# The last attention's scores as three f32r products of high and low parts, with fewer slots

## The reference

```python
q = _split_heads(xn @ Wq)                      # 16 heads of 64
kv = xn @ Wkv
k = _split_heads(kv[..., :INNER]); v = _split_heads(kv[..., INNER:])
mem = _split_heads(memories @ Wm)              # memories: the context
k = jnp.concatenate([k, mem], axis=2)          # 100 own keys + 722
v = jnp.concatenate([v, mem], axis=2)
dots = jnp.einsum('bhid,bhjd->bhij', q, k) * scale
attn = jax.nn.softmax(dots, axis=-1)
out = jnp.einsum('bhij,bhjd->bhid', attn, v)
return out.transpose(0, 2, 1, 3).reshape(b, n, h * d) @ Wo + bo
```

## Time and profile before

| | us |
|---|---|
| median of three runs | 1789.09 |
| the profiled execution | 1776.6 |
| its span | 1774.9 |
| TensorE matmuls busy | 1598.0 (90%) |
| TensorE weight loads busy | 1370.2 (77%) |
| VectorE busy | 1088.9 (61%) |
| ScalarE busy | 787.0 (44%) |
| GpSimd busy | 185.0 (10%) |

### The profile page before, as it was taken

One profiled execution on the slowest core, in us unless ns is written; L12 is line 12 of the kernel. 1 busy time (PEld: TensorE's weight loads), 2 busy tenths in 40 slices (PEclk: granted clock), 3 DMA queues, 4 the chain that ended last, 5 costly groups with the idle time before them and its releaser, 6 DMA issues. The chain is left out here.

```text
span 1774.9 us, 31782 instructions
## 1 busy us (share of the span) xinstructions
PE 1598.0 (90%) x11904; PEld 1370.2 (77%) x11904; DVE 1088.9 (61%) x2045; ACT 787.0 (44%) x1418; POOL 185.0 (10%) x172
## 2 busy tenths in 40 slices
PE   6998399999999399799999999999999749999990
PEld 5786289988888399588787787878787449999990
DVE  3687567777777633246565565656565557767774
ACT  2445255555555332144444354535444325445541
POOL 1103201111111101100000000000000030011003
PEclk9998599999999799899999999999999869999995
DMA  6995356666667434231110112021112046666643
GB/s 192 370 401 196 103 216 216 219 213 204 216 205 236 131 114 145 87 102 34 35 49 23 50 27 58 19 58 36 40 36 75 11 147 210 203 205 197 219 158 90
DMA packets 93125, 246.00 MB, mean 139 GB/s; under 512 B 32870, under 2 KB 39526, under 8 KB 77926
## 3 DMA queue, kind: packets, MB, share of 16 engines
q1 hardware_dynamic: 82534, 219.87, 36.7%
q0 software_dynamic: 10496, 24.81, 5.9%
HBM read 179.14 MB, written 65.50 MB: 138 GB/s over the span
## 5 line engine op out<-in xcount | busy, mean ns | idle before, releaser
L1848 PE MATMUL banks<-a_ch,a_wm 128*128 128x362 f32 (+1 forms) x1024 | 285.7, 340 | 9.4 <-DVE a_cl L2009 9.4
L1172 DVE TENSOR_TENSOR e_lo<-e_raw,e_hi 128x2048 fp32r<-128x2048 f32 x98 | 225.5, 2301 | 91.1 <-ACT e_hi L1250 91.0
L1123 PE MATMUL banks<-e_xh,e_hi 128*128 128x256 f32 x768 | 215.9, 281 | 4.2 <-DVE e_xl L1188 4.2
L1123 PE MATMUL banks<-e_xl,e_hi 128*128 128x256 f32 x768 | 215.7, 281 | 0.0
L1123 PE MATMUL banks<-e_xh,e_lo 128*128 128x256 f32 x768 | 215.2, 280 | 0.0
L1250 ACT CAST e_hi<-e_raw 128x2048 fp32r<-128x2048 f32 x98 | 186.5, 1903 | 29.0 <-PE banks L1102 29.0
L1848 PEld LDWEIGHTS banks<-a_ch,a_wm 128*128 128x128 f32 x1024 | 186.2, 190 | 11.1 <-DVE a_cl L2009 10.5
L1848 PE MATMUL banks<-a_cl,a_wm 128*128 128x362 f32 (+1 forms) x512 | 168.8, 330 | 0.0
L2022 DVE TENSOR_REDUCE a_nmax<-banks 100x1 f32<-100x822 f32 x128 | 123.5, 1007 | 72.2 <-PE banks L1882 72.2
L1102 PE MATMUL banks<-e_hi,e_hh 128*128 128x512 f32 x384 | 153.8, 400 | 1.5 <-DVE e_hl L1208 1.5
L1123 PEld LDWEIGHTS banks<-e_xh,e_hi 128*128 128x128 f32 x768 | 145.1, 189 | 10.6 <-issue 4.6
(11 more groups left out here) (270 smaller groups left out, 3052.4 us busy)
## 6 DMA issues: line engine op xcount, KB each, us to landing
e_raw<-wout SPq DMA_DIRECT2D x50, 1024.0 KB, 15.5
e_raw<-w SPq DMA_DIRECT2D x34, 1024.0 KB, 22.4
slot_rows<-a_zero SPq DMA_DIRECT2D x66, 514.0 KB, 9.8
e_raw<-wgate SPq DMA_DIRECT2D x17, 1024.0 KB
e_raw<-wup SPq DMA_DIRECT2D x17, 1024.0 KB, 4.9
a_craw<-ctxT SPq DMA_DIRECT2D x32, 361.0 KB, 6.4
e_xs<-slot_rows SPq DMA_DIRECT2D x18, 514.0 KB, 3.7
p_raw<-Wkv SPq DMA_DIRECT2D x4, 1024.0 KB, 12.0
```

The lines of the kernel that those rows point to most:

```text
L1123: mm = nc.tensor.matmul(ps[:, bank, 0:CAP], w[:, cc, cut], x[:, cc, :], start=t == 0, stop=t == len(terms) - 1)
L1172: nc.vector.tensor_tensor(lo[g % 2][i], raw[q % RAW][:], hi[g % 2][i].bitcast(F32), ALU.subtract)\
L1848: mm = nc.tensor.matmul(ps[:, 6 + half, 0:wide], w[:, cc, cut], x[:, cc, start:start + wide], start=cc == 0 and t == 0, stop=cc == DC - 1 ...
```

## The change

The scores are taken as three f32r products: high part by high part, high by low, low by high, all three for one width before the next width, the heads in turn. For this the pair's queries and keys are kept as a high and a low tile of 100 + 822 columns (`qk_hi`, `qk_lo`), in two slots. The projected rows stand once more in f32 (`mem`), from which `turn_values` reads. New work for each pair:

- GpSimd (`own_split`): a copy of the own queries and keys (128x200) to the high tile, and the subtraction that makes the low part. SyncE loads them to a tile of their own (`own_qk`), two pairs ahead where it was three.
- ScalarE: in `keys` the first half of the projected rows is copied out of the bank twice, to the high tile and to `mem`; `keys_second`, after the values' copies, makes the high part of the second half out of `mem`.
- VectorE (`keys_low`): after `keys` it waits for the high part and subtracts 128x722.

Values and probabilities have three slots in place of four. GpSimd's routing work is now spread over the steps, behind the step's `own_split`.

```diff
-    SLOTS = 4
+    QK_SLOTS, V_SLOTS, P_SLOTS = 2, 3, 3
+    MEMORY = 2 * T
...
+                def own_queries_keys(p):
                     if not exists(p):
                         return
-                    after(sp, sc, p - SLOTS + 1)
...
+                    b, m, s = p // IC, p % IC, p % QK_SLOTS
+                    after(sp, own_lo, p - QK_SLOTS + 1)
+                    sp.dma_start(own_qk[s][:, 0, :], s1.q[b, :, m, :]).then_inc(qk_in[s], 16)
+                    sp.dma_start(own_qk[s][:, 1, :], s1.kk[b, :, m, :]).then_inc(qk_in[s], 16)
+
+                def own_values(p):
+                    if not exists(p):
+                        return
+                    b, m, s = p // IC, p % IC, p % V_SLOTS
+                    after(sp, yd, p - V_SLOTS + 1)
+                    sp.dma_start(v[s][0:T, 0, :], s1.v[b, :, 128 * m:128 * m + 128]).then_inc(v_in[s], 16)
...
-                    own(b, m + SLOTS - 1)
+                    own_queries_keys(IC * b + m + 2)
+                    own_values(IC * b + m + 2)
...
+                def own_split(p):
+
+                    s = p % QK_SLOTS
+                    raw = own_qk[s][:].rearrange("p a t -> p (a t)")
+                    pool.wait_ge(qk_in[s], 32 * (p // QK_SLOTS + 1))
+                    after(pool, sc, p - QK_SLOTS + 1)
+                    pool.tensor_copy(qk_hi[s][:, 0:MEMORY], raw).then_inc(own_hi, 1)
+                    pool.wait_ge(own_hi, p + 1)
+                    pool.tensor_tensor(qk_lo[s][:, 0:MEMORY], raw, qk_hi[s][:, 0:MEMORY].bitcast(F32), ALU.subtract)\
+                        .then_inc(own_lo, 1)
...
+                def step(b, u, m):
+                    p = IC * b + m
+                    if exists(p + 2):
+                        own_split(p + 2)
+                    if m == STATS_AT and b >= 1:
+                        route_root(b - 1)
+                    if m == RANK_AT and b >= 1:
+                        route_store(b - 1)
...
                     for f, (first, wide) in enumerate(WIDE):
-                        for two in range(2):
-                            r = slice(HD1 * two, HD1 * two + HD1)
-                            mm = nc.tensor.matmul(ps[0:T, 2 * two + f, 0:wide], q[s][r, :],
-                                                  kT[s][r, first:first + wide], start=True, stop=True)
+                        for t, (x, y) in enumerate(((hi, hi), (hi, lo), (lo, hi))):
+                            for two in range(2):
+                                r = slice(HD1 * two, HD1 * two + HD1)
+                                mm = nc.tensor.matmul(ps[0:T, 2 * two + f, 0:wide], x[r, 0:T],
+                                                      y[r, T + first:T + first + wide], start=t == 0, stop=t == 2)
                     mm.then_inc(sc, 1)
...
+                def keys_low(p):
+
+                    s = p % QK_SLOTS
+                    dve.wait_ge(k_v, p + 1)
+                    dve.wait_ge(k_a, p + 1)
+                    dve.wait_ge(k_h, p + 1)
+                    nc.vector.tensor_tensor(qk_lo[s][:, MEMORY:], mem[s][:], qk_hi[s][:, MEMORY:].bitcast(F32),
+                                            ALU.subtract).then_inc(k_l, 1)
...
-                    nc.scalar.copy(kT[m % SLOTS][:, T + start:T + start + wide], ps[:, 6, 0:wide]).then_inc(k_a, 1)
+                    hi = qk_hi[p % QK_SLOTS]
+                    nc.scalar.copy(hi[:, MEMORY + start:MEMORY + start + wide], ps[:, 6, 0:wide])
+                    nc.scalar.copy(mem[p % QK_SLOTS][:, start:start + wide], ps[:, 6, 0:wide]).then_inc(k_a, 1)
+
+                def keys_second(p):
+
+                    s = p % QK_SLOTS
+                    act.wait_ge(k_v, p + 1)
+                    start, wide = HALF[1]
+                    nc.scalar.copy(qk_hi[s][:, MEMORY + start:MEMORY + start + wide], mem[s][:, start:start + wide])\
+                        .then_inc(k_h, 1)
...
                         values(p + 1, (m + 1) % IC)
+                    if exists(p + 2):
+                        keys_second(p + 2)
```

More of the change, by code:

```diff
@@ L1706, in attend @@
         cl = [k.sb(c, f"a1_cl{u}", [128, DC, S], F32R) for u in range(2)]
-        q = [k.sb(c, f"a1_q{u}", [128, T]) for u in range(SLOTS)]
-        kT = [k.sb(c, f"a1_kT{u}", [128, KEYS]) for u in range(SLOTS)]
-        v = [k.sb(c, f"a1_v{u}", [128, len(KB1), 128]) for u in range(SLOTS)]
-        P = [k.sb(c, f"a1_P{u}", [T, KEYS]) for u in range(4)]
+        own_qk = [k.sb(c, f"a1_own{u}", [128, 2, T]) for u in range(QK_SLOTS)]
+        qk_hi = [k.sb(c, f"a1_qk_hi{u}", [128, T + KEYS], F32R) for u in range(QK_SLOTS)]
+        qk_lo = [k.sb(c, f"a1_qk_lo{u}", [128, T + KEYS], F32R) for u in range(QK_SLOTS)]
+        mem = [k.sb(c, f"a1_mem{u}", [128, S]) for u in range(QK_SLOTS)]
+        v = [k.sb(c, f"a1_v{u}", [128, len(KB1), 128]) for u in range(V_SLOTS)]
+        P = [k.sb(c, f"a1_P{u}", [T, KEYS]) for u in range(P_SLOTS)]
         PT = [k.sb(c, f"a1_PT{u}", [128, len(KB1), T]) for u in range(2)]
@@ L1728, in attend @@
         ch_done, cl_done = k.sem("a1_ch_done"), k.sem("a1_cl_done")
-        qk_in = [k.sem(f"a1_qk_in{s}") for s in range(SLOTS)]
-        v_in = [k.sem(f"a1_v_in{s}") for s in range(SLOTS)]
+        qk_in = [k.sem(f"a1_qk_in{s}") for s in range(QK_SLOTS)]
+        v_in = [k.sem(f"a1_v_in{s}") for s in range(V_SLOTS)]
+        own_hi, own_lo = k.sem("a1_own_hi_ready"), k.sem("a1_own_lo_ready")
         pj, k_a, k_v = k.sem("a1_projected"), k.sem("a1_keys_act"), k.sem("a1_keys_dve")
+        k_h, k_l = k.sem("a1_keys_hi_ready"), k.sem("a1_keys_lo_ready")
         vt, v_done = k.sem("a1_values_turned"), k.sem("a1_values_copied")
@@ L1793, in _ @@
                     context(0, cc)
-                for m in range(SLOTS - 1):
-                    own(0, m)
+                for p in range(2):
+                    own_queries_keys(p)
+                    own_values(p)
                 sp.dma_start(s1.wo[:], a["Wo"].rearrange("(c p) n -> p c n", p=128)).then_inc(o_in, 16)
@@ L1817, in _, with route_root, route_store @@
                                    base=0, pattern=[[1, T]], channel_multiplier=-1).then_inc(made_more, 1)
-                for b in range(B):
+                def own_split(p):
[7 more added lines that the diff above has]
+                        .then_inc(own_lo, 1)
+                def route_root(b):
                     pool.wait_ge(va, b + 1)
                     pool.tensor_tensor(rs[:, b:b + 1], rs[:, b:b + 1], k.nhalf[:, 0:1], ALU.pow).then_inc(rstd, 1)
+                def route_store(b):
                     pool.wait_ge(slotted, b + 1)
@@ L1828, in _ @@
                             .then_inc(scattered2 if j else scattered[b % 2], 16)
+                def step(b, u, m):
[6 more added lines that the diff above has]
+                        route_store(b - 1)
+                for p in range(2):
+                    own_split(p)
+                over_steps(pool, step)
+                route_root(B - 1)
+                route_store(B - 1)
                 pool.wait_ge(scattered2, 16 * B)
@@ L1893, in turn @@
                         mm = nc.tensor.transpose(ps[0:size, 4 + n // 5, T * (n % 5):T * (n % 5) + T],
-                                                 P[(2 * m + two) % 4][:, first:first + size], k.ident[0:T, 0:T])
+                                                 P[(2 * p + two) % P_SLOTS][:, first:first + size], k.ident[0:T, 0:T])
                     mm.then_inc(pt, 1)
                 def attended(p, b, m):
-                    s = m % SLOTS
+                    s = p % V_SLOTS
                     pe.wait_ge(pt_a, p + 1)
@@ L2015, in keys @@
                     start, wide = HALF[1]
-                    nc.vector.tensor_copy(kT[m % SLOTS][:, T + start:T + start + wide], ps[:, 7, 0:wide])\
+                    nc.vector.tensor_copy(mem[p % QK_SLOTS][:, start:start + wide], ps[:, 7, 0:wide])\
                         .then_inc(k_v, 1)
+                def keys_low(p):
[5 more added lines that the diff above has]
+                                            ALU.subtract).then_inc(k_l, 1)
                 def highest(p, m, two):
@@ L2029, in normalise @@
                     dve.wait_ge(ri, 2 * p + two + 1)
-                    nc.vector.tensor_scalar(P[h % 4][:], P[h % 4][:], rinv[:, h:h + 1], None, ALU.mult)\
+                    to = P[(2 * p + two) % P_SLOTS]
+                    nc.vector.tensor_scalar(to[:], to[:], rinv[:, h:h + 1], None, ALU.mult)\
                         .then_inc(pn, 1)
```

28 lines of the change are left out of this document (10 added, 18 removed).

## The result

| | before | after |
|---|---|---|
| median (four runs each) | 1789.68 | 1777.43 |
| the profiled execution | 1776.6 | 1778.84 |
| its span | 1774.9 | 1777.1 |
| first scores in the trace | 764.0 | 778.5 |
| first scores to last scores | 627.5 | 614.1 |

The kernel after is faster: ratio 0.9930, with an interval of 0.9918 to 0.9942, which is 12.3 us (10.4 to 14.7). The forecast was 1774.9, range 1767 to 1797. The two profiled executions say the opposite of the medians, 1776.6 against 1778.8.

The account below looks back on a forecast made before the run. TensorE's own list was taken to bound the last attention's loop; 57 of 64 steps gaining 0.25 us make 14.2, so the median 1789.1 falls to 1774.9 us, with helpers' work hidden; range 1767 to 1797.

Parts of the forecast that it names:

- What bounds: Last attention's loop of 64 pairs: goes at the pace of TensorE's own list, matmuls covering 79.46 of 80 us.
- The scores' phase: TensorE, first scores' weight load to that of the next phase: from 1.56 to 1.31 us, 0.25 less a step.
- Rival 3: Scores reach the f32 pace per column: phase 1.21 us, gain 19.4, 1769.7 us; lower edge of the forecast's 0.70 chance.
- The overlap: Scores on TensorE: two heads' f32r products on different 64 rows run side by side; without any overlap, 0.87 us lost.
- rival 1: Scores on TensorE: the two heads' halves do not overlap in f32r, 1841 us; chance 0.16, whole or in part.
- 57 steps gain, the late ones not: 57 of 64 steps gain 0.25, 14.2 us; the step after the routing's logits, one a batch, grows 0.1 at most.
- rival 2: GpSimd and VectorE get in each other's way, 17 us eating the gain, 1792; chance 0.14 with lesser lateness of helpers.
- the last pair's 0.25: Tail of the last attention: the last pair also gains 0.25 us, counted in the 57 steps.
- The helpers: New work a pair: ScalarE two 0.47 us operations, VectorE 0.91, GpSimd two of 0.6 to 1.6 each; hidden in plain steps.
- Slots: Values' loads two pairs ahead with three slots wait for the same product as three ahead with four: no cost.
- The sum: Profiled execution 1776.6 less 14.2 gives 1762.4 us; the same step off the median 1789.1 gives 1774.9.

Follow-up runs that it names:

- two_products: The changed kernel without the scores' product of low queries by high keys: 1748.59 against 1778.78 us for the kernel before, ratio 0.9829.
- same_rows: The changed kernel with both heads' scores taken from head 0's rows, in a single execution: 1848.25 against 1789.02 us for the kernel before.
- heads_outer: The changed kernel with all three score products of one head listed before the other's: 1765.42 against 1778.78 us for the kernel before, ratio 0.9926.
- three_slots: The kernel before with three slots in place of four, three probability tiles and loads two pairs ahead: 1789.61 against 1788.66 us, ratio 1.0005.
- f32_scores: The changed kernel with scores as one f32 product of the high parts, all helper work kept: 1779.22 against 1778.78 us for the kernel before, ratio 1.000.
- splits_earlier: The changed kernel with the next context's four splits one step earlier in the batch: 1765.47 against 1778.78 us for the kernel before, ratio 0.9922.
- before_splits: The kernel before with splits a step earlier and behind the output's additions, without f32r scores: 1784.82 against 1788.66 us, ratio 0.9971.

## Why the prediction was right, step by step

**What bounds.** Right: undoing the scores alone brings the plain steps back to 8.91 to 8.98. The steps follow TensorE's list. That the whole time came back to 1.000 too is in part the clock of the last batch.

**The scores' phase.** Predicted 1.31 us, measured 1.29; gain 0.25 predicted, 0.27 measured. The pace was taken from products on 128 rows and held on 64 rows: 0.376 for a pair of products of both widths, by two_products, where 0.375 was predicted. Only the remainder was 0.16 and not 0.18. Rival 3, the f32 pace per column, fell: 1.21 was its mark. The Trainium skill (TensorE: Matmul & The Clock Gate, "Back-to-back issue gap") gives 0.216 for 512 columns; the scores' loads are 0.23 apart, so the row decided rightly.

**The overlap.** Right, and it was the dearest assumption: without it the time is 1848 (measured) where rival 1 was given 1841. The forecast rested on the halves' places, and same_rows (a single execution) and heads_outer show that the places alone carry it. The Trainium skill, Part 3 of the same page ("Packing small matmuls"), has products on different rows run together; for f32r these two runs now show it.

**57 steps gain, the late ones not.** The steps that gain do it in full. The late ones were to stand still or grow by 0.1 at most, and they grew by 0 to 0.44, 1.3 us in sum. The step that failed is the one that looked only at `keys_low` ahead of the routing; it did fit, five times of six. What was missed is VectorE's small operations, which grow by up to 0.30 in sum, by the trace beside GpSimd's `own_split`. That interference was priced as rival 2, for the scaling in plain steps, where it found room, and not where no room was. The balance of the trace: 56 of the 63 distances are shorter, by 0.262 in the mean, 14.7 in all; less the 1.3 of the late ones that is the 13.4 from first to last scores, where 14.2 were predicted with the last pair's 0.25 in them. So two small misses of opposite sign meet in the sum: 0.26 a step where 0.25 was taken, and the late steps' 1.3 where nothing was.

**The helpers.** VectorE 0.91 us a pair as predicted, ScalarE's two copies 0.46 and 0.51 (0.47 each), GpSimd's 0.35 and 0.62 when alone (0.6 each). All hidden in plain steps. TensorE's waits at L1906, the line that L1869 has become, are 7.2 us in sum up to the last batch, where the earlier trace rows have 4.5, and under the 10 that the prediction allowed:

```profile
PEld banks L1906 <- ACT a_mem L2188: 7.2, 6, 1.4
PE banks L1906 <- DVE a_PT L2085: 5.6, 6, 1.2
```

Six waits of about 1.2, one for each late step, and none in a plain step. The last batch adds one of 2.6, which was 2.3 before. Both names are in place: in the step shown above ScalarE's copy L2188 ends at 1072.26 and VectorE's L2085 at 1072.35, and the later one decides.

**Slots.** Right for three (three_slots).

**The sum.** It went from the profiled 1776.6 to 1762.4 and on to the median by a constant. The two medians differ by 12.3 (10.4 to 14.7), the trace's stretch by 13.4, the forecast by 14.2; what is over is the late steps and the measurement's width.

## What to carry to other kernels

Price a product from the distance of starts, and decide whether two products overlap from the rows they sit on, not from their order in the list (tested here for two heads of 64 rows each). New work on an idle engine is free where the bounding engine's releases come with room and costs in the step where they come late, so look for that step first, and ask there what runs beside the new work. In a hand-written list put work that is ready ahead of a wait (the output's additions ahead of the split): with the split a step earlier this was worth another 6 to 9 us against the changed kernel.

## What the hardware showed that I had not expected

**Order doesn't matter for products on different rows.** The fourth product of the list started 10 ns after the first (heads_outer, 1014.08 x2), phase 1.30 against 1.29. The Trainium skill (TensorE: Matmul & The Clock Gate, Part 3, "What overlaps and what doesn't") has matmuls start strictly in the order of the program. By this trace the fourth starts ahead of the second (1014.39), so the rule doesn't hold here between products on different rows, and the measurement decides.

**Small VectorE operations feel GpSimd too, reductions don't.** L187 on 100x8 went from 0.23 to 0.45 us beside a 128x200 subtraction, and the scaling of 100x822 from 0.65 to 0.73 in the mean with three subtractions; GpSimd's own subtraction went from 0.62 to 0.88 at 1017.05 of after. The reductions beside it kept their time, 0.16 on 100x8 and 1.00 on 100x822, and so did the copies out of the banks.

**The same instructions took another time in another set of runs.** The kernel before had a median of 1778.78 on the chip of the first runs (f32_scores, heads_outer, two_products, splits_earlier) and of 1788.66 to 1789.68 in the other sets, on other chips. The profiled executions differ ahead of the changed stage: first scores at 764.0 to 769.4 us in the executions on the first chip, 775.4 to 778.8 in the others, where the list of instructions up to there is the same. Busy time from 220 to 290 us, in before and then in after:

```profile
220.00:290.00 70.00, 69.81 (x453) 63.65 (x454) 49.04 (x73) 39.09 (x47) 5.33 (x2) 0.98 0.68 230
```

```profile
220.00:290.00 70.00, 59.98 (x374) 54.66 (x375) 43.00 (x65) 36.10 (x47) 4.14 (x3) 0.87 0.58 201
```

Before is further on in its list (453 products against 374), with 230 against 201 GB/s and a granted clock of 0.98 against 0.87. It isn't the change: in this window the executions on the first chip have 433 to 452 products, all of changed kernels, and the others 371 to 387, two of them (three_slots, before_splits) without the f32r scores. Before's profiled execution looks like those of the first chip, which would explain that it lay 12.5 us under its median; what makes the difference is open, and since the first chip was used in one set alone, chip and moment aren't told apart. So profiled executions were compared here only by a stretch of their own, and times only on one chip.
